# A fused two-layer decoder on one core: another VectorE order in the first attention, norms and scatters spread over later stage borders, and the causal mask copied into the score bank by ScalarE

## The reference

```python
x = x + _L0_attn_ref(_layernorm(x), wq, bq, wk, bk, wv, bv, wo, bo, ln_g, ln_b)
x = x + _L0_xattn_ref(_layernorm(x), ctx, ctx, Wh, wg_w, wo_w, gn_gamma, gn_beta)
x = x + _L0_ffn_ref(_layernorm(x), ln_gamma, ln_beta, bases, slopes, output_scale)
x = x + _L1_attn_ref(_layernorm(x), w_qkv, w_out)
x = x + _L1_xattn_ref(_layernorm(x), mask, ctx, ctx, wq, wk, wv, wo)
x = x + _L1_ffn_ref(_layernorm(x), sw1, swg, sw2, rw1, rwg, rw2, Wg, Wdown, Wup, biases)
```

```python
residual = h
x = (h - mu) * jax.lax.rsqrt(var + EPS) * ln_g + ln_b
q, k, v = x @ wq.T + bq, x @ wk.T + bk, x @ wv.T + bv    # per head
attn = einsum('bihd,bjhd->bhij', rope(q), rope(k)) * scale
attn = softmax(where(causal, -inf, attn))
return einsum('bhij,bjhd->bihd', attn, v) @ wo.T + bo + residual
```

```python
onehot = tile_idx[None, :] == arange(64)[:, None]
tile_min = where(onehot, tok_min, inf).min(axis=1)       # and tile_max
u = clip((x_slice - mn) / (mx - mn + 1e-08), 0.0, 1.0 - 1e-06)
delta = (b + s * x_local) * output_scale[tile_idx][:, None]
out = zeros_like(xf).at[arange(N)[:, None], tok_dims].set(delta)
```

## Time and profile before

| | |
|---|---|
| median of 3 runs | 1173.4 us (1173.1 to 1173.42) |
| profiled execution, its own time | 1175.98 us |
| its span (first to last instruction) | 1173.8 us |
| mean granted TensorE clock, share of full | 0.951 |
| first attention | 0 to 586 us |
| retention, spline | to 673, to 745.5 us |
| window, cross, mixture | to 929, to 1012, to the end |
| TensorE, VectorE, ScalarE, GpSimd busy over the span | 87, 68, 61, 27 % |

### The profile page before, as it was taken

The page is one execution under the profiler, slowest core; times in us unless marked ns, Lnnn a source line. Parts: engine busy times, 40 slices in busy tenths (PEclk is TensorE's granted clock), DMA queues, the critical chain, the costliest instruction groups (busy, mean ns, idle before and its releaser), DMA issues. The chain is left out here.

```text
span 1173.8 us, 18988 instructions
## 1 busy us (share of the span) xinstructions
PE 1025.9 (87%) x6729; PEld 845.1 (72%) x6757; DVE 792.9 (68%) x1456; ACT 715.6 (61%) x1969; POOL 318.4 (27%) x244
## 2 busy tenths in 40 slices
PE   5989889999999989999688867389999599598997
PEld 4878778887888878898677656267776499474555
DVE  5788867668576686777556777777777534365774
ACT  5777656776667766667433364187777244456883
POOL 2444323233233333332201010144444200101442
PEclk9999999999999999999989977599999799799999
DMA  6211000000000010000070000000000000006342
GB/s 198 73 54 54 1 1 1 2 1 1 2 1 1 1 32 1 1 2 1 1 203 1 1 1 1 0 1 2 2 2 2 1 1 2 13 2 143 100 108 72
DMA packets 31980, 31.79 MB, mean 27 GB/s; under 512 B 8336, under 2 KB 23440, under 8 KB 31888
## 3 DMA queue, kind: packets, MB, share of 16 engines
q1 hardware_dynamic: 31888, 30.60, 9.4%
HBM read 28.36 MB, written 2.23 MB: 26 GB/s over the span
## 5 line engine op out<-in xcount | busy, mean ns | idle before, releaser
L330 POOL TENSOR_TENSOR roped_q<-roped_q,sin_q 128x512 f32<-128x512 f32 x64 | 81.9, 1280 | 328.9 <-DVE sin_q L467 328.9
L380 ACT ACTIVATE P<-banks,neg_max 128x128 f32<-128x128 f32 x256 | 90.5, 370 | 38.7 <-DVE neg_max L490 38.7
L330 POOL TENSOR_TENSOR roped_k<-roped_k,sin_k 128x512 f32<-128x512 f32 x64 | 99.1, 1548 | 44.8 <-DVE sin_k L467 44.8
L1512 ACT ACTIVATE win_P<-banks,win_neg_max 128x128 f32<-128x128 f32 x256 | 91.3, 383 | 31.0 <-DVE win_neg_max L1578 30.5
L407 ACT ACTIVATE oT_hi<-banks,bv_col 128x512 fp32r<-128x512 f32 x64 | 44.1, 689 | 86.7 <-PE banks L613 86.7
L1471 POOL TENSOR_TENSOR win_P<-win_P,win_inv 128x512 f32<-128x512 f32 x64 | 66.7, 1042 | 100.5 <-DVE win_inv L1583 100.2
L592 PE MATMUL banks<-WO_lo,oT_hi 128*128 128x256 f32 x256 | 75.6, 295 | 11.5 <-DVE oT_lo L493 11.4
L613 PE MATMUL banks<-PT,V 128*128 128x128 f32 x512 | 70.6, 281 | 16.3 <-ACT PT L403 16.3
L389 ACT ACTIVATE sin_k<-banks 64x512 f32<-64x512 f32 x128 | 75.9, 593 | 8.2 <-PE banks L37 6.4
L389 ACT ACTIVATE sin_q<-banks 64x512 f32<-64x512 f32 x128 | 76.0, 594 | 4.5 <-PE banks L37 2.2
L613 PEld LDWEIGHTS banks<-PT,V 128*128 128x128 f32 x512 | 62.7, 193 | 20.7 <-ACT PT L403 20.7
(11 more groups left out here) (378 smaller groups left out, 3223.8 us busy)
## 6 DMA issues: line engine op xcount, KB each, us to landing
moe_gate_of<-moe_gate_rows SPq DMA_DIRECT2D x32, 256.0 KB, 4.1
X<-in_x SPq DMA_DIRECT2D x4, 512.0 KB, 7.5
stage<-in_wqT SPq DMA_DIRECT2D x4, 512.0 KB, 3.9
stage<-in_wvT SPq DMA_DIRECT2D x4, 512.0 KB, 5.7
stage<-in_woT SPq DMA_DIRECT2D x4, 512.0 KB, 4.0
ctx<-in_ctxT SPq DMA_DIRECT2D x4, 512.0 KB, 7.5
out<-X SPq DMA_DIRECT2D x8, 256.0 KB, 2.8
stage<-in_wkT SPq DMA_DIRECT2D x3, 512.0 KB, 3.8
```

Source lines behind the costliest of these rows:

```text
L330: nc.gpsimd.tensor_tensor(roped[w][:, p, :], roped[w][:, p, :], sin_part[w][:], ALU.add).then_inc(roped_sum[w], 1)
L380: ins = nc.scalar.activation(P[:, i, :], SC[:, i * 128:(i + 1) * 128], ACT.Exp, bias=neg_max[:, r % 2, i:i + 1], accum_out=exp_sum[:, r % ...
L1512: ins = nc.scalar.activation(P[:, h % 2, s, i, :], SC[2 * (h % 2) + s][:, i * 128:(i + 1) * 128], ACT.Exp, bias=neg_max[:, h % 2, at:at + ...
```

## The change

It has four parts. Nothing is changed in what is computed, except that the look-up of the extremes goes by three bf16 parts of each value.

1. The mask. Only the first step still multiplies it into SC. For every later step ScalarE copies it there (lay_mask), right behind the exponentials of the step before, and the scores wait for that copy.
2. VectorE's order in the first attention. Splitting weights, normalising, splitting X^T, the residual and the last group's norm stand between oT_lo and the reciprocal; some tables of r are one smaller. The first four V blocks of a group, from the second group on, are projected at r = 14 and 15 of the group before.
3. Spline. VectorE normalises all batches, twelve of them from norms that retention has finished; the strided reductions become folding additions; tables are looked up in bf16; ScalarE makes the "off" tile and rounds the window's weights, VectorE splits them. At the end the result goes into X by four instructions of 64 columns a batch (scatter), for batches 0 to 3 only.
4. Later borders. Batches 4 to 15 are scattered inside the window stage; the norms of the first batches of window, cross and mixture are finished in the stage before; clears and constants go to GpSimd and ScalarE.

```diff
+        def v_at(r, g):
+            if g == 0 and r < 2:
+                return [(0, 2 * r), (0, 2 * r + 1)]
+            return [((r + 2) // 4, (r + 2) % 4)] if r < 14 or g + 1 < NG else []
...
+                def lay_mask():
+                    nc.scalar.activation(SC[:].rearrange("p (a n) -> p a n", a=GROUP), four(mask[:]), ACT.Copy).then_inc(mask_laid, 1)
...
                         ins.then_inc(exps_done, 1)
+                        if u + 1 < STEPS:
+                            act.wait_ge(exps_done, u + 1)
+                            lay_mask()
...
                     if u == 0:
                         pe.wait_ge(consts_made, 3)
-                    nc.tensor.matmul(SC[:], ident_b[:], four(mask[:]), start=True, stop=True)
+                        nc.tensor.matmul(SC[:], ident_b[:], four(mask[:]), start=True, stop=True)
+                    wait(pe, mask_laid, u)
...
+                    if g == 0:
+                        for i in split_at(r):
+                            split_weights(i)
+                    if g + 1 < NG and r in prepared_at(g):
+                        normalise((g + 1) * GROUP + prepared_at(g).index(r))
+                    if g + 1 < NG and r == PREPARED + 1:
+                        split_xT(g + 1)
+                    if g < NG and r >= HEADS0 - GROUP and not (g == 0 and r == 12):
+                        add_h(g * GROUP + r - (HEADS0 - GROUP))
                     if live(u, STEPS):
                         dve.wait_ge(exps_done, u + 1)
...
+                    for m in (128, 64, 32):
+                        link(TT(wide[:, some, 0:m], wide[:, some, 0:m], wide[:, some, m:2 * m], ALU.add))
...
                 for b in range(B):
-                    ins = nc.tensor.matmul(bank[2][:, 2 * b:2 * b + 2], hotT[:, b, :], ext_table[:], start=True, stop=True)
+                    ins = nc.tensor.matmul(bank[2][:, 6 * b:6 * b + 6], hotT_b[:, b, :], ext_parts[:].rearrange("p a e -> p (a e)"), start=True, stop=True)
...
+def scatter(nc, X, hot, delta, b):
+    for j in range(4):
+        columns = X[:, b, :].rearrange("p (t j) -> p t j", j=4)[:, :, j]
+        ins = nc.vector.scalar_tensor_tensor(columns, hot[:, b, :], delta[:, b, j:j + 1], columns, ALU.mult, ALU.add)
+    return ins
...
+                for b in range(GROUP):
+                    scatter(nc, X, hot, delta, b).then_inc(scattered, 1)
+                for b in range(GROUP):
+                    dve.wait_ge(scattered, b + 1)
+                    nc.vector.bn_stats(stats[:, b, :], X[:, b, :]).then_inc(next_stat, 1)
...
+                    if h < 3:
+                        finish_batch(11 + h)
+                    if h == 2:
+                        finish_batch(14)
+                        finish_batch(15)
+                        finish_norms(slice(HALF, B), 12 + 7, stat)
```

More of the change, by code:

```diff
@@ L205, in phase_attn0 @@
         scored = sem("scored")
+        mask_laid = sem("mask_laid")
         max_found = sem("max_found")
@@ L1190, in _ @@
                         take_found(p)
+                    if i == 0:
+                        nc.scalar.activation(kept["win_w_hi"][:], w["win_w_in"][:], ACT.Copy).then_inc(win_rounded, 1)
+                        for g in range(2):
+                            take_hot_b(g)
                 act.wait_ge(high_known, 1)
@@ L1193, in _ @@
                     place_high(b)
+                for g in range(2, NG):
+                    take_hot_b(g)
                 for b in range(HALF, B):
@@ L1217, in _ @@
+                dve.wait_ge(rstd12_ready, 1)
                 dve.wait_ge(stat, n)
[L1218 to L1224 removed]
@@ L1225, in _ @@
[L1225 to L1229 removed]
+                normalise(3)
                 def choose(i):
@@ L1298, in _ @@
                 link(TT(coef[:, 2], coef[:, 2], coef[:, 0], ALU.add))
-                link(TT(coef[:, 3], coef[:, 2], over(found[:, :, 128], W), ALU.mult))
+                link(TT(delta[:], coef[:, 2], over(found[:, :, 128], W), ALU.mult))
                 dve.wait_ge(residual_ready, B)
-                for g in range(NG):
-                    some = slice(g * GROUP, (g + 1) * GROUP)
-                    for j in range(W):
-                        ins = TT(tiles(wide[:, some, :])[:, :, :, j], hot[:, some, :], over(coef[:, 3, some, j], NT), ALU.mult)
-                    link(ins)
-                    link(TT(X[:, some, :], X[:, some, :], wide[:, some, :], ALU.add))
-                    for b in range(some.start, some.stop):
-                        nc.vector.bn_stats(stats[:, b, :], X[:, b, :])
+                for b in range(GROUP):
[3 more added lines that the diff above has]
+                    nc.vector.bn_stats(stats[:, b, :], X[:, b, :]).then_inc(next_stat, 1)
+                dve.wait_ge(next_stat, GROUP)
+                finish_stats(nc, dve, next_stat, GROUP, stats[:, FIRST, :], mean[:, FIRST], var_eps[:, FIRST], ln_tmp[:, :, FIRST], LN_EPS)
             @block.tensor
```

330 lines of the change are left out of this document (188 added, 142 removed).

## The result

The changed kernel takes 1154.1 us in the median of four runs (1152.6 to 1155.2), before 1173.4 (1173.1 to 1173.6): the ratio is 0.9835, with a 95% interval of 0.9818 to 0.9852. It is faster, by 19 us (1.65%) and not by 41; 1154.1 lies above the range that was given (1119 to 1150). The profiled execution has a span of 1152.7 us against 1173.8.

What follows compares the result with a forecast made beforehand. TensorE was taken to bound attention groups 1 to 3, with losses at group borders from VectorE's order. Attention -26.8, retention and spline -12.0, window +2.1, cross -2.3, mixture -2.1 sum to -41.1: 1132 us, range 1119 to 1150.

Steps and rivals of the forecast that it cites:

- Fifteen border intervals: Attention steps around the group borders: all at 7.82 us, 140.2 to 117.3 in sum, -22.9, including the V move.
- the ring: ScalarE's shortest loop without a pause in an attention step: 7.03 us with a V copy, 7.66 with the 0.63 mask copy.
- the cover by TensorE: Attention steps: TensorE's 7.82 us hides ScalarE's 7.66; gone where ScalarE has more to do, such as evacuation at 8.46.
- group 0: First attention group, taken as bound by weight rounding on ScalarE and VectorE: -1.0 us, between 0 and eleven times 0.22.
- the ordinary steps: Eleven intervals each of groups 1 and 2, plus +1.0 in group 3: +2.9 us; group 3's other twelve: -5.8.
- The window: Window stage: head saves 3.9 us, deferred scatters expose 5.5 and a finish 0.5; +2.1 in all, bounds -2 and +9.
- Rival D: Window stage: deferred scatters are not hidden and collide with GpSimd, 6 to 14 us back, 1138 to 1146; chance 0.15.
- The rule of the page: Small scatters: 58 fixed cycles plus elements gives 0.13 us for 64 columns, 2.0 for sixteen; sum 0.7 lower.
- B: Attention: ScalarE's mask write to the bank costs 0.9 to 1.1 us, 10 to 26 back, 1142 to 1158; chance 0.15.
- C: Attention: mask copy so dear ScalarE bounds every step; slower than before from 1.5 us a copy; chance 0.03.
- E: Group borders: moved V products wait for late split X^T, borders keep 3 us each, 1142; chance 0.05.
- Retention, spline, cross and mixture: Later stages: retention and spline together -12.0 us, including -11.9 at the spline's end; cross -2.3, mixture -2.1.

Runs made afterwards that it cites:

- e10: Kernel before with only VectorE's new order in the first attention, early splits as before in the first two steps: 1143.3 us, ratio 0.973.
- e9: Changed kernel with ScalarE copying the mask into the score bank twice in every step: 1185.5 us, ratio 1.009 to before.
- e5: Changed kernel with the mask a TensorE product again and the first two steps' weight splits behind the rotary products: 1130.6 us, ratio 0.962 to before.
- e3: Kernel before with only the mask copied into the score bank by ScalarE: 1204.6 us, ratio 1.026.
- e6: e5 with scatter batches 14 and 15 and their norm spread over later ticks, window zero tile on ScalarE: 1127.1 us, ratio 0.959 to before.

## Why the prediction was wrong

**The direction and the borders were right.** Fifteen border intervals were put at 7.82 and take 7.94 in the mean. That the residual work ahead of the row maximum held them is confirmed by e10. But part of the reason given was wrong: of the 21.2 the order alone makes 19.3 (e10), and the V move, put into the same term, 1.2.

**"With 0.63 the ring is 7.66, just under the 7.82 of TensorE": the price was right, what it was set against was not.** This is the step that failed: the cover by TensorE was worked out for the plain steps and taken for the first group too. The copy was forecast as free or as a gain there. The runs show that it costs 6.3 us in that group's first eleven intervals, and 12 to 15 us over the attention. The start of the copy to the start of the next instruction is 0.63 (64.09 to 64.72), and the short interval of a later group is 7.66. The failure is in group 0 ("between 0 and eleven times 0.22 I take -1.0") and in the ordinary steps. Group 0's steps stood on ScalarE's ring once VectorE was out of the way: the order gave 7.4 us in those eleven intervals and the copy took 6.3 back, and the two errors met in -1.1. In groups 1 to 3 the +2.9 was 7.8: the first interval of a group takes 8.54 and not 7.8, the ones with evacuation 8.7 to 8.8 and not 8.46, and one takes 10.34 at a dip of the clock. As parts: VectorE's order -33.5, V -1.2, the copy +15.5 (12.1 without the dips), where I had priced order and copy together in each step and never the copy by itself. Priced by itself, the copy would have shown that most of the 41 us came from one part, with the copy as a debt.

**The start, +5.2, was not in the sum.** "The work now stands where VectorE waits for the exponentials anyway": in the steps 0 and 1 there are none, so the wait for a rounded weight stands ahead of the rotary products. It is the question that the prediction asks of a cover (what if it is gone) and did not ask of these two steps.

**The window, +2.1 forecast and +10.3 measured.** (Over all profiles with either form of the stage the difference is 5 to 12, in the mean 7.) A batch was priced at 1.1 us and takes 1.45: sixteen instructions take 3.94 us, 0.246 each, not the 0.17 that I took "back to back with overlap"; the row's 0.23 alone was the better guide. The place then decided: three batches in one tick, ahead of a reciprocal. "Clears that go to GpSimd cost nothing" failed too: VectorE's first two tiles took 2.23 us together beside the clear of V, and 0.74 without it. Rival D gave about the right size for the window, by collisions that hardly happened: that is luck.

**The rule of the page.** The estimate of 0.13 us for 64 elements, from the Trainium skill, "VectorE: DVE Perf Modes", section on the TRN2 errata, was too low: one lasts 0.31 to 0.34, and the measured pace is 0.246. The tile beside the clear (1.9 us instead of 0.4, while the clear ran for 1.81) agrees with the Trainium skill, "SBUF — State Buffer", section "Who interferes with whom": a VectorE instruction in a two-port mode, which that page says tensor_scalar can enter, and a GpSimd instruction exclude each other, and the later one waits for the whole of the other. The one long scatter, issued 0.07 us after a multiplication of 1.05 on GpSimd had begun, agrees with the same section's rule for two SBUF inputs, which the prediction names. But three scatters beside GpSimd's power of 128x4 took 0.33 to 0.34 and were not held.

**The rivals.** B's mechanism (ScalarE's ring) decided, but not through its dearer write: the copy takes 0.60, as a copy out of a bank. That B's range, 1142 to 1158, holds the measured time is luck. C's break-even was too generous: with the gain that was really there, one more 0.63 a step turned faster into slower (e9). E did not happen. Retention, spline, cross and mixture came within 1 us of their sums, the spline with two errors that met: its end fell by 11.0 us and not by 11.9, since the sixteen scatters take 3.94 and not 2.7, and what stands ahead of it fell by 1.3 where 0.2 was forecast.

With both attention cures (e5) the kernel is at 1130.6, close to the forecast of 1132. That is luck too: its attention gains 34.7 us where 26.8 were forecast, and its window stage loses 8 where 2.1 were.

## What to carry to other kernels

Moving an operation off the engine that is full is worth what the interval says after the move, in every kind of step: write down each engine's ring for each kind (first steps, preparing steps, last steps), add the piece to it, and sum the kinds. When an edit holds several parts, price each by itself, since a debt is hidden in a sum that comes out negative anyway. Work "moved under a wait" has to be checked in the steps that have no such wait, and work that is put off should be dealt out one piece at a time, behind whatever the next engine waits for.

## What the runs showed of the hardware

The clock fell beside two short stalls. Shorter stretches of the changed kernel's window stage (columns as in the earlier trace rows):

```profile
729.60:733.80 4.20, 1.69 (x12) 1.48 (x12) 4.13 (x13) 1.65 (x4) 0.47 (x1) 1.00 0.00 0
733.80:736.50 2.70, 2.61 (x19) 1.90 (x20) 2.31 (x6) 0.00 (x0) 0.00 (x0) 0.75 0.00 0
736.50:739.50 3.00, 2.47 (x15) 1.35 (x12) 2.51 (x9) 2.71 (x14) 0.91 (x1) 0.50 0.01 3
739.50:742.50 3.00, 2.93 (x13) 2.81 (x14) 2.98 (x7) 2.19 (x12) 1.18 (x2) 0.50 0.00 0
...
751.30:754.60 3.30, 0.00 (x0) 0.00 (x0) 3.13 (x16) 0.00 (x0) 0.61 (x1) 0.64 0.00 0
754.60:757.50 2.90, 2.86 (x18) 2.18 (x19) 2.76 (x5) 1.51 (x8) 1.32 (x2) 0.50 0.00 0
```

In the head TensorE is idle for more than half of 4.2 us, while VectorE scatters batches 8 and 9 ahead of the split of k; then the clock falls from 1.00 (2.4 GHz) to 0.50 (1.2 GHz) and stays there through the second tick, where TensorE is nearly always busy. The full stop in tick 2 is followed by the same. All seven profiles that have the head and the ticks of the changed kernel show it. The kernel before and e10 have a clock of 1.00 in all of their first ticks. But e3, with the same window stage, has 0.67 and 0.68 in two of its first four intervals, and they take 19.3 us instead of 16.4:

```profile
790.40:809.70 19.30, 17.16 (x137) 13.12 (x138) 11.65 (x22) 14.38 (x70) 7.28 (x7) 0.82 0.01 1
```

So such a dip comes without these stalls too, and that the stalls make the clock fall is not shown. What it costs can be read where the work is the same: 2.9 us there, and 2.3 us behind the last row maximum of the window stage, in e5 and then in e6:

```profile
873.40:889.30 15.90, 9.32 (x104) 6.43 (x103) 10.01 (x18) 4.48 (x18) 3.12 (x3) 1.00 0.00 1
```

```profile
867.00:885.20 18.20, 11.63 (x104) 8.45 (x104) 10.04 (x18) 4.48 (x18) 3.12 (x3) 0.81 0.00 1
```

What share of the 9.6 us that the first four intervals lost is clock and what is waiting was not measured apart. Smaller things: a ScalarE copy of 128x512 into a score bank takes 0.60 us, the same as out of one, and a clear on GpSimd stretched a VectorE tensor_scalar of 0.4 us to 1.9.
